# A state-space convolution on one core: x1 loads three channels ahead and late in SyncE's turn, Toeplitz loads first in it, k and B ahead of the transposes

## The chip, the cores and the metric

One core of one Trainium2 chip runs the whole program. The metric is the device time of one execution in microseconds (us), as the median of three runs. TensorE is called PE here, VectorE DVE, ScalarE ACT, GpSimd POOL and SyncE SP, as in the profile.

## The reference: what is computed

x has 128 batches, 128 channels and 2048 steps. Two residual layers follow each other:

```python
W = weights[condition]                      # (128, 128, 128): one of 16 matrices for each batch
x1 = x + jnp.einsum('bct,bcd->bdt', x, W)
mask = jnp.arange(L) < length[:, None]      # per batch
K = 2.0 * jnp.einsum('hn,hnl->hl', Cs, jnp.exp(P)).real     # (128 channels, 2048)
y = causal convolution of (x1 * mask) with K, channel by channel   # by FFT in the reference
out = x1 + (y + x1 * mask * D[:, None]) * mask
```

Everything is float32.

## The kernel before

**Rows.** The first layer works batch by batch ("rows"): 512 KB of x are loaded into `row_x`, multiplied by the matrix of the batch's condition (`w_sel`), copied to `row_y` and stored to `x1_scratch` in DRAM. The time axis is cut into two segments of 1024 steps. The 128 rows of segment 0 and four of segment 1 are made ahead of everything else. The other 124 rows of segment 1 are made one at a time beside the channels of segment 0 (`row_in_parts` on PE, `halve_w`, `halve_x` and `take_row` on ACT, `split_row` on POOL).

**Channels.** The second layer works channel by channel: 128 turns for segment 0, then 128 for segment 1. A turn k loads the channel's 128 batches x 1024 steps from `x1_scratch` into one of four tiles (512 KB, `load_x1`), transposes them on PE (`turn`), and splits them into a high and a low part (`keep_u` on ACT, `split_u` on DVE). PE then makes the chunk states from them (`drive`, `advance`), the near part with a Toeplitz matrix (`from_chunk`, with `t_hi`, `t_lo` and `toep`) and the far part from the states (`from_state`). `take_y` on DVE puts the result into the tile under the mask, and `store_x2` writes the tile to `out`. Tile, Toeplitz, b_mat and row_x buffers come in fours; `load_x1` waits for the store of the channel that had the tile four turns earlier.

**Matrices.** In segment 0 the kernel's taps k and the matrix B of channel k+2 are made in turn k: `make_mats` on PE, `keep_k`, `halve_k`, `split_k` on DVE, then `store_kernel` writes the taps to DRAM (72 KB). `load_toeplitz` reads them back in skewed form, three loads of 128, 128 and 64 KB, and waits for the landing of that store. B is split (`keep_b` on ACT, `split_b` on DVE) and stored by `store_b` (256 KB) for segment 1, which loads it with `load_b`. The last state of segment 0 goes to `edge_scratch` (line 402) and comes back by `load_edge` in segment 1.

**Order.** Each engine runs a list written out by hand, one turn after the other, and waits on semaphores. SP's list is also the order of the DMA queue on which all transfers but the `x1_scratch` stores (ACT's queue) are issued. A wait in SP's list holds up everything behind it. Which matrix a row needs is read by `act.value_load` into a register of ACT's sequencer (line 536).

Of the kernel before, what the change touches and what calls it, by code (L numbers as in the profile page):

```python
# [31 lines left out]
NCOND = 16  # L32
# [37 lines left out]
def s4d_program(nc, x, cond, length, weights, log_dt, c_in, log_a_real, a_imag, d_in, const_in, out):  # L70
# [10 lines left out]
    with ctx:  # L81
# [215 lines left out]
        def _(sp):  # L297
# [78 lines left out]
            for k in range(2):  # L376
                load_x1(0, k, k, 0)
# [3 lines left out]
            def channels(g, seg, with_rows):  # L381
                for j in range(SLOTS):
# [3 lines left out]
                    if then:  # L386
                        load_x1(then[0], then[1], j2, then[2])
                    if after and after[0] == 0:
                        if not (isinstance(k, int) and k == 0):
                            store_b(k + 1, j1)  # L390
                        load_toeplitz(0, k + 1, j1, after[2])
# [4 lines left out]
                    if with_rows and not (isinstance(g, int) and k + 3 >= B - AHEAD):  # L396
                        load_row(k + ROWS_FIRST + 3, j3, 1, k + AHEAD + 3)
                    if then and then[0] == 0:
                        store_kernel(k + 2, j2)
                    if seg == 0:  # L400
                        sp.wait_ge(s_ready, states_before(0, k) + NCH)
                        sp.dma_start(edge_dram[bass.ds(k, 1), :, :].rearrange("a n b -> (a n) b"), edge[j % 2][:, :]).then_inc(edge_saved[j % 2], 16)
# [107 lines left out]
        def _(act):  # L510
# [22 lines left out]
            def halve_w(m, j):  # L533

                n = m + ROWS_FIRST
                which = act.value_load(cond_sb[0:1, bass.ds(n, 1)], min_val=0, max_val=NCOND - 1)
# [87 lines left out]
            halve_w(0, 0)  # L624
# [3 lines left out]
            def channels(g, seg, with_rows):  # L628
                for j in range(SLOTS):
# [5 lines left out]
                    next_row = with_rows and not (isinstance(g, int) and k + 1 >= B - AHEAD)  # L635
                    keep_s(seg, k, j, 1)
                    if next_row:
                        halve_w(k + 1, j1)
                        halve_x(k + 1, j1, 0)
# [23 lines left out]
        def _(dve):  # L663
# [156 lines left out]
            def channels(g, seg, with_rows):  # L820
                for j in range(SLOTS):
# [7 lines left out]
                    if third:  # L829
                        mats(third[0], k + 3, (j + 3) % SLOTS)  # L830
                    if after:
                        split_u(k + 1, j1, 0)
                    if then and then[0] == 0:
                        keep_k(k + 2, j2)
# [18 lines left out]
        def _(pe):  # L853
# [99 lines left out]
            def channels(g, seg, with_rows):  # L953
                for j in range(SLOTS):
# [8 lines left out]
                    for c in range(NCH):  # L963
# [5 lines left out]
                        if c - 1 >= 1 - seg:  # L969
                            from_state(seg, k, j, c - 1)  # L970
                        if c == 0 and after:
# [3 lines left out]
                        if c == 0 and then and then[0] == 0:  # L975
                            make_mats(k + 2, j2)
# [50 lines left out]
```

## Time and profile before

| | us |
|---|---|
| median of 3 runs | 2345.85 |
| the runs | 2344.41 to 2353.0 |
| the profiled execution's own time | 2358.94 |
| its span, first to last instruction | 2357.1 |

The rows ahead of the channels take about 385 us of the span, segment 0 of the channels goes on to about 1510 us, and segment 1 fills the rest. PE is busy for 92% of the span, DVE 72%, ACT 64%, POOL 50%. The profiled execution is 13 us above the median of the runs.

### The profile page before, as it was taken

The numbers are of one execution on the slowest core, as the hardware profiler recorded it, in microseconds if no ns is written. First come the engines' busy times: TensorE is split into PE (matmuls) and PEld (weight loads), VectorE is DVE, ScalarE is ACT, GpSimd is POOL, SyncE is SP. The second block draws the span as 40 slices with busy tenths as digits, with TensorE's granted clock in tenths as the row PEclk, the third lists the DMA queues.
The fourth block names the chain that finished last, engine by engine and source line by source line (L and its number), as shares of the span: only waits on it lengthen the run. The fifth ranks groups of instructions, "written<-read, shape, count | busy, mean of one in ns | idle before, by whom it ended". The sixth has DMA issues, their size and how long they took to land.

```text
span 2357.1 us, 61717 instructions
## 1 busy us (share of the span) xinstructions
PE 2174.2 (92%) x15101; PEld 1880.7 (80%) x15101; DVE 1699.5 (72%) x3359; ACT 1505.9 (64%) x4354; POOL 1175.0 (50%) x1862
## 2 busy tenths in 40 slices
PE   6777778999999999999999999899999999999999
PEld 2222226888888888888888888799999999999998
DVE  4999204777777777777777777677777777777776
ACT  4556556777777777777777777455555555555555
POOL 0994503666666666666666666333333333333331
PEclk9999999999999999999999999999999999999999
DMA  8999999999999999999999999889989999899887
GB/s 319 420 414 369 394 359 330 316 315 315 314 316 318 317 317 318 320 315 317 320 319 311 323 316 307 241 251 262 268 253 267 266 270 259 259 261 264 254 260 223
DMA packets 337444, 716.26 MB, mean 304 GB/s; under 512 B 39554, under 2 KB 170884, under 8 KB 337412
## 3 DMA queue, kind: packets, MB, share of 16 engines
q1 hardware_dynamic: 300548, 581.66, 79.7%
q10 hardware_dynamic: 36864, 134.23, 14.0%
q8 instruction: 13, 0.21, 0.0%
q14 instruction: 19, 0.16, 0.0%
HBM read 395.92 MB, written 319.82 MB: 304 GB/s over the span
## 4 chain that ended last, share of the span: by engine, by line
PE 36%; DMA 28%; DVE 9%; SPq 8%; issue 8%; ACT 6%; ACTq 4%; DVEq 0%; POOL 0%
DMA decay<-x_scratch 12%; DMA toep<-k_scratch 11%; PE bank L900 7%; PE bank L902 6%; PE bank L901 6%; DMA row_x<-in_x 5%; PE bank L882 4%; DVE decay L803 4%; PE bank L945 4%; PE bank L869 3%; PE bank L937 3%; SPq L339 3%; SPq L355 2%; DVE e_lo L786 2%; ACTq L521 2%
## 5 line engine op out<-in xcount | busy, mean ns | idle before, releaser
L791 DVE TENSOR_TENSOR u_lo<-bank,u_hi 128x512 fp32r<-128x512 f32 x512 | 352.2, 688 | 252.7 <-ACT u_hi L603 246.7
L797 DVE TENSOR_TENSOR s_lo<-state,s_hi 128x128 fp32r<-128x128 f32 x768 | 291.8, 380 | 236.7 <-ACT s_hi L615 235.4
L900 PE MATMUL bank<-t_hi,u_hi 128*128 128x256 f32 x1024 | 361.7, 353 | 43.1 <-DMA toep<-k_scratch 42.5
L612 ACT ACTIVATE state<-bank 128x128 f32<-128x128 f32 x768 | 213.9, 279 | 286.8 <-PE bank L902 149.5
L803 DVE COPY_PREDICATED decay<-mask,bank 128x512 f32<-128x512 uint8 x512 | 379.1, 741 | 23.8 <-PE bank L902 3.6
L945 PE MATMUL bank<-toep,u_odd 128*128 128x128 f32 x2048 | 392.8, 273 | 0.0
L546 ACT ACTIVATE row_y<-bank 128x512 f32<-128x512 f32 x512 | 301.4, 589 | 138.2 <-ACT row_y L546 38.7
L489 POOL TENSOR_TENSOR x_lo<-row_x,x_hi 128x256 fp32r<-128x256 f32 x496 | 371.5, 778 | 0.0
L869 PE MATMUL bank<-row_x,w_sel 128*128 128x512 f32 x528 | 265.5, 630 | 94.2 <-DMA row_x<-in_x 50.2
L466 POOL TENSOR_TENSOR outer<-par 128x256 f32<-128x256 f32 x512 | 321.5, 649 | 20.5
L463 POOL COPY par<-table 128x71 f32 (+1 forms) x256 | 62.4, 244 | 540.4 <-PE bank L902 540.4
L945 PEld LDWEIGHTS bank<-toep,u_odd 128*128 128x128 f32 x2048 | 314.0, 189 | 0.0
L900 PE MATMUL bank<-e_hi,s_hi 128*128 128x256 f32 x896 | 307.3, 343 | 0.0
L869 PEld LDWEIGHTS bank<-row_x,w_sel 128*128 128x128 f32 x528 | 93.3, 195 | 263.7 <-ACT row_y L546 143.9
L603 ACT ACTIVATE u_hi<-bank 128x512 fp32r<-128x512 f32 x512 | 301.9, 590 | 0.0
L901 PE MATMUL bank<-t_lo,u_hi 128*128 128x256 f32 x1024 | 288.6, 282 | 0.0
L902 PE MATMUL bank<-t_hi,u_lo 128*128 128x256 f32 x1024 | 288.3, 282 | 0.0
L486 POOL TENSOR_TENSOR w_lo<-w_sel,w_hi 128x128 fp32r<-128x128 f32 x124 | 57.2, 461 | 423.0 <-ACT x_hi L529 423.0
L937 PE MATMUL bank<-state,r_mat 128*128 128x128 f32 x1280 | 265.5, 289 | 0.5 <-ACT state L612 0.4
L900 PEld LDWEIGHTS bank<-t_hi,u_hi 128*128 128x128 f32 x1024 | 195.8, 191 | 81.7 <-DMA toep<-k_scratch 65.7
L882 PE MATMUL bank<-eye_r,tile_r 128*128 128x128 f32 x2048 | 225.4, 253 | 34.1 <-DMA decay<-x_scratch 33.0
L615 ACT ACTIVATE s_hi<-state 128x128 fp32r<-128x128 f32 x768 | 238.6, 311 | 24.2
(139 smaller groups left out, 5456.6 us busy)
## 6 DMA issues: line engine op xcount, KB each, us to landing
row_x<-in_x SPq DMA_DIRECT2D x256, 512.0 KB, 6.1
x_scratch<-row_y ACTq DMA_DIRECT2D x256, 512.0 KB, 5.6
decay<-x_scratch SPq DMA_DIRECT2D x256, 512.0 KB, 6.4
out<-decay SPq DMA_DIRECT2D x256, 512.0 KB, 4.4
b_scratch<-b_mat SPq DMA_DIRECT2D x128, 256.0 KB, 6.5
t_hi<-k_scratch SPq DMA_DIRECT2D x256, 128.0 KB, 4.7
t_lo<-k_scratch SPq DMA_DIRECT2D x256, 128.0 KB, 4.4
b_mat<-b_scratch SPq DMA_DIRECT2D x128, 256.0 KB, 5.0
```

What stands on the lines that cost most here:

```text
L466: pool.tensor_tensor(outer[:, n, :].rearrange("p (a b) -> p a b", b=LOW), par[j][:, p0:p0 + LOW].unsqueeze(2).to_broadcast([P, LOW, LOW]), ...
L489: last = pool.tensor_tensor(x_lo[i][:, cols], row_x[j][:, cols], x_hi[i][:, cols].bitcast(fp32), ALU.subtract)
L603: nc.scalar.activation(u_hi[j % 2][:, 4 * q:4 * q + 4, :], blocks, ACT.Copy).then_inc(u_half, 1)
L791: v.tensor_tensor(u_lo[j % 2][:, blocks, :], t_bank[q][:, :].rearrange("s (k b) -> s k b", b=B), u_hi[j % 2][:, blocks, :].bitcast(fp32), ...
L803: v.copy_predicated(tile[j][:, cols], mask[:, seg * SEG + q * BANK:seg * SEG + (q + 1) * BANK], y_bank[q][:, :]).then_inc(y_taken, 1)
L869: mm(to_bank[:, :], w_sel[j][:, :], row_x[j][:, q * BANK:(q + 1) * BANK], start=True, stop=True).then_inc(row_made, 1)
L882: ins = nc.tensor.transpose(t_bank[q][:, n * P:(n + 1) * P].bitcast(fp32r), tile_r[j][:, at:at + P], eye_r[:, :])
L900: mm(to, w_hi, m_hi, start=start, stop=False, skip_group_check=True)
L901: mm(to, w_hi, m_lo, start=False, stop=False, skip_group_check=True)
L902: return mm(to, w_lo, m_hi, start=False, stop=stop, skip_group_check=True)
L937: mm(s_bank[j % 2][:, c * P:(c + 1) * P], r_mat[j][:, :], whole[:, :], start=False, stop=True, skip_group_check=True).then_inc(s_made, 1)
L945: mm(y[:, P:CHUNK], u_odd[i][:, c, :], toep[j][:, P - 1::-1], start=False, stop=True, skip_group_check=True)
```

## The change

SP: `load_x1` moves from the front of a turn to a place behind the kernel store, ahead of the edge and of `store_x2`, and loads the channel three ahead in place of two; three of them are issued ahead of the first turn. `load_toeplitz` comes first in a turn of segment 0, and `store_b` goes behind the row load. ACT: the condition is read ahead of the first state's copy. DVE: `keep_k` comes ahead of the first `split_u`. PE: `make_mats` comes ahead of the transposes. No work is added or removed.

```diff
--- before.py
+++ after.py
@@ -373,7 +373,7 @@
                 rows(g, 1)
             load_toeplitz(0, 0, 0, 0)
             sp.wait_ge(par_ready, 1)
-            for k in range(2):
+            for k in range(3):
                 load_x1(0, k, k, 0)
             for n in range(ROWS_FIRST, ROWS_FIRST + 3):
                 load_row(n, n % SLOTS, 1, n - B)
@@ -383,11 +383,7 @@
                     k = g * SLOTS + j
                     after, then, third = (later(g, j, seg, d) for d in (1, 2, 3))
                     j1, j2, j3 = ((j + d) % SLOTS for d in (1, 2, 3))
-                    if then:
-                        load_x1(then[0], then[1], j2, then[2])
                     if after and after[0] == 0:
-                        if not (isinstance(k, int) and k == 0):
-                            store_b(k + 1, j1)
                         load_toeplitz(0, k + 1, j1, after[2])
                     if then and then[0] == 1:
                         load_toeplitz(1, k + 2, j2, then[2])
@@ -395,8 +391,12 @@
                         load_b(k + 3, j3)
                     if with_rows and not (isinstance(g, int) and k + 3 >= B - AHEAD):
                         load_row(k + ROWS_FIRST + 3, j3, 1, k + AHEAD + 3)
+                    if after and after[0] == 0 and not (isinstance(k, int) and k == 0):
+                        store_b(k + 1, j1)
                     if then and then[0] == 0:
                         store_kernel(k + 2, j2)
+                    if third:
+                        load_x1(third[0], third[1], j3, third[2])
                     if seg == 0:
                         sp.wait_ge(s_ready, states_before(0, k) + NCH)
                         sp.dma_start(edge_dram[bass.ds(k, 1), :, :].rearrange("a n b -> (a n) b"), edge[j % 2][:, :]).then_inc(edge_saved[j % 2], 16)
@@ -530,10 +530,13 @@
                 if q == NQ - 1:
                     ins.then_inc(row_halved, 1)
 
-            def halve_w(m, j):
+            def condition_of(m):
+
+                return act.value_load(cond_sb[0:1, bass.ds(m + ROWS_FIRST, 1)], min_val=0, max_val=NCOND - 1)
+
+            def halve_w(m, j, which):
 
                 n = m + ROWS_FIRST
-                which = act.value_load(cond_sb[0:1, bass.ds(n, 1)], min_val=0, max_val=NCOND - 1)
                 act.wait_ge(row_made, n * NQ - NQ)
                 w = w_all[:, bass.ds(which, 1), :].rearrange("c k d -> c (k d)")
                 nc.scalar.activation(w_sel[j][:, :], w, ACT.Copy)
@@ -621,7 +624,7 @@
 
             for q in range(NQ):
                 keep_u(0, 0, q)
-            halve_w(0, 0)
+            halve_w(0, 0, condition_of(0))
             for q in range(NQ):
                 halve_x(0, 0, q)
 
@@ -633,9 +636,11 @@
                     if seg == 1:
                         halve_edge(k, j, g)
                     next_row = with_rows and not (isinstance(g, int) and k + 1 >= B - AHEAD)
+                    if next_row:
+                        which = condition_of(k + 1)
                     keep_s(seg, k, j, 1)
                     if next_row:
-                        halve_w(k + 1, j1)
+                        halve_w(k + 1, j1, which)
                         halve_x(k + 1, j1, 0)
                     if after:
                         keep_u(k + 1, j1, 0)
@@ -828,10 +833,10 @@
                     third = later(g, j, seg, 3)
                     if third:
                         mats(third[0], k + 3, (j + 3) % SLOTS)
+                    if then and then[0] == 0:
+                        keep_k(k + 2, j2)
                     if after:
                         split_u(k + 1, j1, 0)
-                    if then and then[0] == 0:
-                        keep_k(k + 2, j2)
                     split_s(seg, k, j, 2)
                     if then and then[0] == 0:
                         halve_k(k + 2, j2)
@@ -968,12 +973,12 @@
                         from_chunk(k, j, c)
                         if c - 1 >= 1 - seg:
                             from_state(seg, k, j, c - 1)
+                        if c == 0 and then and then[0] == 0:
+                            make_mats(k + 2, j2)
                         if c == 0 and after:
                             pe.wait_ge(x1_loaded[j1], after[2] * 16 + 16)
                             for q in range(NQ):
                                 turn(k + 1, j1, q)
-                        if c == 0 and then and then[0] == 0:
-                            make_mats(k + 2, j2)
                         if with_rows and c % 2:
                             row_in_parts(k, j, c // 2)
                     from_state(seg, k, j, NCH - 1)
```

In segment 0 SP's turn looks so before; `decay` is the tile that `load_x1` fills, `x_scratch` is what it reads. The rows are those of one turn near the end of the rows, from one store of `out` to the next.

```order
L324 DMA decay<-x_scratch 128x1024 [waits x2_stored2]
L355 DMA b_scratch<-b_mat 128x512 [waits b_ready]
L339 DMA t_hi<-k_scratch 128x1x256 [waits k_stored1]
L339 DMA t_lo<-k_scratch 128x1x256
L339 DMA toep<-k_scratch 128x1x128
L311 DMA row_x<-in_x 128x1024 [waits row_made]
L329 DMA k_scratch<-k_rows 16x1152 [waits k_ready]
L402 DMA edge_scratch<-edge 128x128 [waits s_ready]
L343 DMA out<-decay 128x1024 [waits y_taken]
```

After the change the same turn reads so. The tile's load has gone from the front to ahead of the edge, the three Toeplitz loads now open the turn, and the b store has gone behind the row's load.

```order
L339 DMA t_hi<-k_scratch 128x1x256 [waits k_stored1]
L339 DMA t_lo<-k_scratch 128x1x256
L339 DMA toep<-k_scratch 128x1x128
L311 DMA row_x<-in_x 128x1024 [waits row_made]
L355 DMA b_scratch<-b_mat 128x512 [waits b_ready]
L329 DMA k_scratch<-k_rows 16x1152 [waits k_ready]
L324 DMA decay<-x_scratch 128x1024 [waits x2_stored3]
L402 DMA edge_scratch<-edge 128x128 [waits s_ready]
L343 DMA out<-decay 128x1024 [waits y_taken]
```

In segment 1 one turn reads so on SP before, from the loop over the groups:

```order
L324 ISA [waits x2_stored2]
L324 DMA decay<-x_scratch 128x1024
...
L339 DMA t_hi<-k_scratch 128x1x256
...
L339 DMA t_lo<-k_scratch 128x1x256
...
L339 DMA toep<-k_scratch 128x1x128
...
L361 ISA [waits y_made]
L361 DMA b_mat<-b_scratch 128x512
...
L351 ISA [waits y_made]
L351 DMA edge<-edge_scratch 128x128
...
L343 ISA [waits y_taken]
L343 DMA out<-decay 128x1024
```

After the change the tile's load stands behind the b load and ahead of the edge's; its wait for the tile's earlier store stands there too, and the edge load and the out store are behind it.

```order
L339 DMA t_hi<-k_scratch 128x1x256
...
L339 DMA t_lo<-k_scratch 128x1x256
...
L339 DMA toep<-k_scratch 128x1x128
...
L361 ISA [waits y_made]
L361 DMA b_mat<-b_scratch 128x512
...
L324 ISA [waits x2_stored3]
L324 DMA decay<-x_scratch 128x1024
...
L351 ISA [waits y_made]
L351 DMA edge<-edge_scratch 128x128
...
L343 ISA [waits y_taken]
L343 DMA out<-decay 128x1024
```

ACT's list at the start of a turn of segment 0 before; TENSOR_LOAD is the read of the condition, and the state's copy is what PE's `advance` and DVE's `split_s` wait for.

```order
L550 DMA x_scratch<-row_y 128x1024
...
L612 ACTIVATE state<-bank 128x128 [waits s_made]
L615 ACTIVATE s_hi<-state 128x128 [waits s_ready]
...
L536 TENSOR_LOAD cond_sb
...
L539 ISA [waits row_made]
L539 ACTIVATE w_sel<-w_all 128x128
L540 ACTIVATE w_hi<-w_all 128x128
...
L529 ACTIVATE x_hi<-row_x 128x512 [waits x_loaded3]
```

After the change the read stands between the row's store and the state's copy, and the two copies of the matrix follow the state directly.

```order
L553 DMA x_scratch<-row_y 128x1024
...
L535 TENSOR_LOAD cond_sb
...
L615 ACTIVATE state<-bank 128x128 [waits s_made]
L618 ACTIVATE s_hi<-state 128x128 [waits s_ready]
...
L542 ISA [waits row_made]
L542 ACTIVATE w_sel<-w_all 128x128
L543 ACTIVATE w_hi<-w_all 128x128
...
L529 ACTIVATE x_hi<-row_x 128x512 [waits x_loaded3]
```

## Rows read from the trace of the kernel before

**Rows 1.** Busy time by stretch: PE, PEld, DVE, ACT, POOL, PEclk, DMA share, GB/s

```profile
100.00:200.00 100.00, 76.54 (x155) 26.05 (x155) 97.48 (x74) 53.64 (x116) 96.75 (x34) 1.00 1.02 409
700.00:1400.00 700.00, 675.36 (x4876) 608.11 (x4875) 529.99 (x1100) 510.98 (x1494) 452.65 (x788) 1.00 0.97 318
1600.00:2300.00 700.00, 678.47 (x5597) 667.98 (x5597) 530.24 (x1076) 408.43 (x1292) 240.00 (x431) 1.00 0.91 262
```

**Rows 2.** Waits in 700:1400: us in total, times, longest

```profile
PE bank L900 <- DMA toep<-k_scratch: 23.8, 38, 1.3
```

**Rows 3.** Waits in 1600:2300

```profile
PE bank L882 <- DMA decay<-x_scratch: 20.5, 29, 1.5
```

**Rows 4.** Issues of the out store in 700:1400, line 343: ns, first, last start

```profile
L343 SPq DMA_DIRECT2D out<-decay x79: 327/332/333, 700.8 to 1395.2; - x79
```

**Rows 5.** The same in 1600:2300, with its time to landing

```profile
L343 SPq DMA_DIRECT2D out<-decay x108: 360/361/361, 1600.6 to 2297.1; - x108
...
DMA to landing us min/median/max: 3.3/3.9/5.2
```

**Rows 6.** Timeline of SP, one turn of segment 0: start us, us

```profile
763.35 0.33 SPq L343 DMA_DIRECT2D out<-decay  x1
763.86 0.64 SPq L324 DMA_DIRECT2D decay<-x_scratch  x1
764.68 1.09 SPq L355 DMA_DIRECT2D b_scratch<-b_mat  x1
766.05 0.58 SPq L339 DMA_DIRECT2D t_hi<-k_scratch  x1
...
769.51 0.34 SPq L329 DMA_DIRECT2D k_scratch<-k_rows  x1
...
772.02 0.33 SPq L343 DMA_DIRECT2D out<-decay  x1
```

**Rows 7.** Timeline of SP, one turn of segment 1

```profile
1898.31 0.36 SPq L343 DMA_DIRECT2D out<-decay  x1
1898.95 0.34 SPq L324 DMA_DIRECT2D decay<-x_scratch  x1
...
1901.80 0.34 SPq L361 DMA_DIRECT2D b_mat<-b_scratch  x1
1903.56 0.33 SPq L351 DMA_DIRECT2D edge<-edge_scratch  x1
1904.45 0.36 SPq L343 DMA_DIRECT2D out<-decay  x1
```

**Rows 8.** Landing of the x1 load, line 324, in 1600:2300

```profile
DMA to landing us min/median/max: 4.7/6.2/7.7
```

**Rows 9.** Landing of the kernel store, line 329, in 700:1400

```profile
DMA to landing us min/median/max: 3.5/4.4/5.3
```

**Rows 10.** Landing of the Toeplitz loads, line 339, in 700:1400

```profile
DMA to landing us min/median/max: 3.6/4.5/5.9
```

**Rows 11.** Landing of the edge load, line 351, in 1600:2300

```profile
DMA to landing us min/median/max: 1.7/3.4/5.4
```

**Rows 12.** Timeline of ACT, segment 0: start us, us, idle before and releaser

```profile
905.65 0.28 ACT L612 ACTIVATE state<-bank 128x128 f32<-128x128 f32 x1 [1.15 <-PE bank L902]
...
907.06 0.31 ACT L539 ACTIVATE w_sel<-w_all 128x128 f32 x1 [0.79 <-issue]
...
909.04 0.28 ACT L612 ACTIVATE state<-bank 128x128 f32<-128x128 f32 x1 [0.20 <-PE bank L937]
```

**Rows 13.** Timeline of PE in the same turn

```profile
907.03 0.89 PE L882 MATMUL bank<-eye_r,tile_r 128*128 128x128 f32 x8
...
908.18 0.61 PE L895 MATMUL bank<-m_mat,e_mat 128*128 128x128 f32 x4
```

**Rows 14.** Timeline of PE where segment 1 begins

```profile
1518.20 0.96 PE L882 MATMUL bank<-eye_r,tile_r 128*128 128x128 f32 x8 [2.33 <-DMA decay<-x_scratch]
...
1528.88 1.16 PE L882 MATMUL bank<-eye_r,tile_r 128*128 128x128 f32 x8 [2.73 <-DMA decay<-x_scratch]
```

## The prediction

> **What bounds the kernel now.** I read the table by stretch first, for which engine is full; then the chain of waits by window, for what it waits for; then SP's timeline and the landings, for how late that is. In both stages of the channels PE is busy for 96 to 97% of the stretch at the full granted clock (1.00, its 2.4 GHz level), DVE for 76% and ACT for 73 and 58% [rows 1]. So PE is the bound, and what it waits for is the loss. In segment 0 that is the Toeplitz loads, 38 times in 79 turns, 23.8 us [rows 2]; in segment 1 it is the tile loaded from x1_scratch, 29 times in 108 turns, 20.5 us [rows 3].
>
> The rows of waits hold only whole gaps, so I take the loss from the period. The out stores of 79 turns of segment 0 are issued from 700.8 to 1395.2: 78 periods of 8.90 us [rows 4]. In segment 1 there are 107 periods in 696.5 us: 6.51 us [rows 5]. A turn without a wait takes 772.02 - 763.35 = 8.67 us in segment 0 [rows 6], and 1904.45 - 1898.31 = 6.14 us in segment 1 [rows 7]. Both are the commonest values of their stage: about half of the periods of segment 0 lie at or under 8.75, and 47 of 107 in segment 1 at or under 6.2, mostly every second one. The loss is 0.23 us x 124 turns = 29 us in segment 0 and 0.36 us x 126 = 45 us in segment 1. Where the segments meet, the tiles come late twice more, by 2.33 and 2.73 us [rows 14]: 5 us. At most 79 us, 3.4%, are to be had.
>
> The DMA engines are the second candidate. In the rows ahead of the channels they never idle, and the table gives a share of 1.02 at 409 GB/s. The channels have 0.97 and 0.91 [rows 1]. Against 1.02 as full, a turn of segment 0 needs 0.97 / 1.02 x 8.90 = 8.46 us of them and one of segment 1 needs 0.91 / 1.02 x 6.51 = 5.81 us. Both are under PE's 8.67 and 6.14, the first by only 2%.
>
> **Segment 1: the x1 load three ahead.** The load goes out 0.6 us behind the out store [rows 7] and lands 6.2 us later in the median, 7.7 at the worst [rows 8], so at 6.8 to 8.3. About half of the periods are lengthened, so the transposes of PE's next turn are due near the median landing, 6.8: there is no slack. Three ahead, there is a whole period more, 6.14 us. Against that stands that the load goes out later: behind the b load, which goes out 3.5 us into the turn [rows 7], and behind the landing of the store that frees the tile, issued at 0 and landing at 3.9, at worst 5.2 [rows 5]. So the load goes out at 4.0 to 5.3 in place of 0.6, and is due at 6.8 + 6.14 = 12.9. With 6.2 us to land it is there at 10.2 to 11.5: slack 2.7 us in the median and 1.4 with a late store, and only a landing that is late as well (1.5 over its median) uses it up. I keep 0.05 us of the 0.36 for such turns: -0.31 x 126 = -39 us. What is queued behind the new wait on SP: the edge load, which goes out at 5.25 [rows 7], and the out store. The wait ends at 4 to 5.3, so both go out as before. The two waits at the seam go too, since their loads are issued a turn earlier: -5 us.
>
> **Segment 0: the Toeplitz loads first.** They now go out 2.7 us into the turn, behind the x1 load and a b store whose issue alone takes SP 1.09 us [rows 6]. Put first, they go out at 0.5, if the kernel store has landed. It goes out at 6.16 (769.51 - 763.35) [rows 6] and lands 4.4 later, at worst 5.3 [rows 9]: 10.6 to 11.5, or 1.9 to 2.8 us into the next turn. Were nothing else changed, they would gain 0.8 us at best. But they also lose what is ahead of them on the queue: 512 KB of x1 and 256 KB of b, 1.9 us at 409 GB/s. Their landing of 4.5 us, at worst 5.9 [rows 10], is largely that queue. Together they land about 2.5 us earlier, against a longest wait of 1.3 [rows 2]. The wait goes. The DMA engines then have 8.46 of 8.67 us to work, so I don't book the whole 0.23: 0.18 x 124 = -22 us.
>
> **The rest.** The condition's read: ACT idles 0.79 us for it behind the state, and 1.15 us ahead of the state, waiting for PE [rows 12]. The read moves into that second gap; with the issue of the row's store in the same gap the state may come up to 0.4 us later. PE takes it only after the transposes and make_mats, 0.89 and about 1.0 us [rows 13], so nothing is booked, and ACT has its copies of u some 0.4 us earlier. PE's swap: the transposes come later by the length of make_mats, about 0.9 us [rows 13], and half of that is paid by the earlier ACT. The next state's copy has 0.20 us of idle time ahead of it [rows 12]. Between 0 and 0.15 us a turn may reach PE (0 to 19 us); I take 0, since the read's gain and the later transposes nearly meet. In DVE the taps' copy comes ahead of u, which uses the time it idles for u. The third x1 load ahead of the first turn delays the row loads behind it by 512 KB at 409 GB/s: +1 us.
>
> **At one place a page weighs otherwise.** The kernel store of 72 KB takes 4.4 us to land [rows 9]. The Trainium skill ("DMA: Bandwidth & Descriptors", "Anatomy of one DMA — SWDGE (gpsimd) path") gives a fixed cost of about 2.0 us plus bytes / 436e3 for one transfer on GpSimd's path, 2.2 us here, which is an estimate for another issuer. By it the store would be home before the turn ends and the Toeplitz loads would go out at 0.5, 2.2 us earlier than before, and by themselves remove the wait; by the row they wait for the store. The sum above goes by the row. No row here shows a lone store of this size.
>
> **Sum.** -39 - 5 - 22 + 1 = -65 us. The profiled execution took 2358.94 us and becomes 2294. It stands 13 us above the median of 2345.85. If the 13 us are of the kind that is removed, the new median is also about 2294 less a few; if they are the profiler's, it is 2281. I take 2286.
>
> **Rivals.**
> - *The DMA engines are the bound of segment 0.* For it: 8.46 of 8.67 us, and never more than a few unhindered turns in a row. Then the wait for Toeplitz loads turns into one for x1 or rows, segment 0 keeps 8.85 to 8.90, and segment 1, more crowded by the late x1 load, gains half: -20 - 5 = 2321. Against it: segment 1 has 11% of their time free. Chance 0.22.
> - *The kernel store's loop becomes the bound (slower).* Kernel store, landing, t_hi, the other loads, b store, next kernel store is a ring once per turn. From t_hi to the kernel store are 3.46 us, and the b store moved in between adds 1.37 (764.68 to 766.05) [rows 6]: 4.8. With 4.4 to land [rows 9] the ring is 9.2 us, over 8.67. If 256 KB of b directly ahead add 0.65 to the landing, it is 9.9: +1.0 x 124 = 124 us against -43 elsewhere, 2427. It decides from 9.25 us on, which is a landing of 4.45. Against it: the landing is time on the queue behind the row's load, and the x1 load and b store no longer stand ahead of these, so the queue is shorter by up to 1.9 us; at the lowest landing of 3.5 [rows 9] the ring is 8.3 and doesn't bind. Chance 0.08.
> - *The edge comes late in segment 1.* It now lies behind 512 KB of x1, 1.3 us at 409 GB/s, on top of 3.4, at worst 5.4 [rows 11]. It goes out at 5.25 and is due two turns' starts later, at about 12: slack 1.4 in the median, none in the worst. If it takes 0.25 us a turn, 2318. Chance 0.07.
> - *The waits are covered by others at once,* so that no part does what it says: 2345. Chance 0.05.
>
> **How the numbers follow.** The forecast has 0.58 and its own range 2267 to 2306: 79 us gained in full from 2346, and half of it. The range for 8 in 10 reaches over the DMA case and the edge: 2264 to 2322. A measurement of this kernel can tell about 0.5% from no change, 12 us: faster means under 2334. Forecast, edge and nearly all of the DMA case are there: 0.86. Within 0.5%: 0.07; slower: 0.07.
>
> **What would show it.** In the new trace the period of segment 0 is 8.70 to 8.75 and that of segment 1 about 6.2. The waits for toep and for decay<-x_scratch are a few us. t_hi goes out under 2 us behind the out store. The kernel store lands in under 4 us; over 4.5 would be the ring. A DMA share near 1.0 in segment 0 with a new wait for a load is the DMA case; a wait for the edge on ACT line 620 or PE's advance, the edge case. The prediction is wrong if PE's unhindered turn grows, by ACT or DVE, above 8.67.

## The result and the profile after

The changed kernel is slower, by 1.5%. Its median is 2383.66 us (four runs, 2378.92 to 2386.69) against 2348.11 us for the kernel before in the same comparison; the ratio is 1.0148, with a 95% interval of 1.0119 to 1.0177. Forecast were 2286 us, with a range of 2264 to 2322.

The profiled execution took 2378.92 us, its span 2377.1. Cut at the issues of the out store, the two spans differ as follows (before, after): up to the first out store 386.8 and 379.6 us; the first 124 turns of segment 0 1104.9 and 1145.0; the next four turns 34.1 and 33.6; the 127 turns of segment 1 828.2 and 815.8. So segment 1 gave back 12.4 us and segment 0 lost 40.1. The 7.2 us ahead of the first out store are no gain that can be read: between kernels whose code there is the same, that stretch took 380 us in one and 394 in another. The medians lie 35.5 us apart and the two spans 20, since the profiled execution of the kernel before was 11 us above its median and that of the changed kernel 5 us below.

The table by stretch, with the columns of [rows 1]; the second stretch starts a little later, since segment 1 does:

```profile
700.00:1400.00 700.00, 652.65 (x4682) 593.33 (x4680) 513.86 (x1060) 491.95 (x1439) 437.06 (x758) 0.99 0.93 304
1620.00:2320.00 700.00, 683.25 (x5635) 666.83 (x5635) 516.78 (x1083) 411.32 (x1301) 238.71 (x433) 1.00 0.88 264
```

In segment 0 every engine and the DMA engines are less busy than in [rows 1]: PE 653 us for 675, the DMA share 0.93 for 0.97. No engine is full, which points to waits that follow each other in a circle. The waits of 700:1400 (us in total, times, longest), where [rows 2] stood:

```profile
PEld bank L905 <- DMA toep<-k_scratch: 57.8, 42, 3.4
ACT u_odd L605 <- PE bank L887: 53.4, 44, 3.7
PE bank L905 <- DMA toep<-k_scratch: 45.7, 45, 2.9
```

PE waits for the Toeplitz loads longer than before, although they now stand first in SP's turn. They go out 3.45 us behind the out store in the median, where it was 2.59. Why they are late stands in SP's own waits, of the same stretch:

```profile
SPq L339 <- DMA k_scratch<-k_rows: 183.7, 73, 3.6
SPq L343 <- DVE decay L808: 30.5, 47, 1.1
SPq L329 <- DVE k_rows L783: 5.2, 9, 1.4
```

In 73 of some 76 turns SP stands at the first Toeplitz load (line 339), 2.5 us each time, until the kernel store of the turn before has landed. The same view of the kernel before shows that its SP hardly ever did:

```profile
SPq L329 <- DVE k_rows L778: 40.2, 71, 1.1
SPq L339 <- DMA k_scratch<-k_rows: 1.3, 3, 0.5
```

One turn on SP's timeline, beside [rows 6] (start us, us):

```profile
908.15 0.33 SPq L343 DMA_DIRECT2D out<-decay  x1
910.38 0.57 SPq L339 DMA_DIRECT2D t_hi<-k_scratch  x1
911.13 0.55 SPq L339 DMA_DIRECT2D t_lo<-k_scratch  x1
911.87 0.54 SPq L339 DMA_DIRECT2D toep<-k_scratch  x1
912.71 0.36 SPq L311 DMA_DIRECT2D row_x<-in_x  x1
913.26 0.35 SPq L355 DMA_DIRECT2D b_scratch<-b_mat  x1
913.87 0.33 SPq L329 DMA_DIRECT2D k_scratch<-k_rows  x1
914.42 0.37 SPq L324 DMA_DIRECT2D decay<-x_scratch  x1
915.47 0.34 SPq L402 DMA_DIRECT2D edge_scratch<-edge  x1
916.97 0.33 SPq L343 DMA_DIRECT2D out<-decay  x1
918.79 0.58 SPq L339 DMA_DIRECT2D t_hi<-k_scratch  x1
```

From t_hi at 910.38 to the kernel store at 913.87 nothing waits: 3.49 us of issuing. The next t_hi goes out at 918.79, 4.92 us after that store. This is one of the shorter turns; the median of the two parts over segment 0 is 3.52 and 5.65 us. And the landings have grown. Those of the kernel store and of the out store in 700:1400, the first of them where [rows 9] stood:

```profile
DMA to landing us min/median/max: 3.7/5.5/6.5
...
DMA to landing us min/median/max: 4.3/7.3/8.0
```

In segment 1 (1620:2320) the wait for the tile, [rows 3], is gone. In its place:

```profile
ACT s_hi L623 <- DMA edge<-edge_scratch: 156.5, 75, 3.2
PEld bank L942 <- DMA edge<-edge_scratch: 30.7, 45, 1.5
PE bank L942 <- DMA edge<-edge_scratch: 16.4, 33, 1.1
```

and on SP:

```profile
SPq L324 <- DMA out<-decay: 154.6, 103, 2.8
```

SP stands at the x1 load for the landing of an out store in nearly every turn, 1.5 us each time, and the edge load and the next out store stand behind it. That landing, where [rows 5] had 3.9 in the median:

```profile
DMA to landing us min/median/max: 4.0/5.0/6.4
```

### The profile page after: what moved, and what is told of

Read it like the earlier page. It is cut to its first block, busy times and chain, and to the rows that moved or that the text cites. A ratio compares the mean times of both kernels' runs of the same rounds, so it can differ in the third digit from the quotient of the medians.

```text
span 2377.1 us, 61746 instructions
## 1 busy us (share of the span) xinstructions
PE 2178.8 (92%) x15101; PEld 1889.3 (79%) x15101; DVE 1685.0 (71%) x3359; ACT 1505.1 (63%) x4354; POOL 1175.6 (49%) x1862
## 4 chain that ended last, share of the span: by engine, by line
DMA 38%; issue 20%; POOL 20%; SPq 9%; PE 6%; ACTq 2%; ACT 2%; POOLq 1%; DVE 0%; DVEq 0%
DMA out<-decay 26%; POOL x_lo L489 10%; DMA k_scratch<-k_rows 6%; POOL outer L466 5%; PE bank L874 4%; DMA row_x<-in_x 4%; POOL e_mat L471 3%; SPq L339 3%; SPq L324 2%; SPq L351 2%; ACTq L521 1%; POOL w_lo L486 1%; ACT row_y L549 1%; DMA x_scratch<-row_y 1%; ACTq L553 1%
## 5 line engine op out<-in xcount | busy, mean ns | idle before, releaser
L802 DVE TENSOR_TENSOR s_lo<-state,s_hi 128x128 fp32r<-128x128 f32 x768 | 271.1, 353 | 261.2 <-ACT s_hi L618 259.6
L605 ACT ACTIVATE u_odd<-bank 128x256 f32<-128x256 f32 x512 | 191.4, 374 | 131.4 <-PE bank L887 130.4
```

Source lines behind the costliest of these rows:

```text
L802: v.tensor_tensor(s_lo[c][:, :], whole[:, :], s_hi[c][:, :].bitcast(fp32), ALU.subtract).then_inc(s_split, 1)
```

## The experiments

Two theories were open, and both are told here by the ring that they name. **Ring one**, segment 0: t_hi, the other Toeplitz loads, the row load, the b store, the kernel store, its landing, and t_hi again. If it sets the time, then the period is the time from t_hi's issue to the kernel store's issue, plus the landing, plus SP's own step. **Ring two**, segment 1: the x1 load waits for the landing of the out store of the turn before; then come the x1 load, the edge load and the next out store. Its rival for segment 1 was a slower engine, and for segment 0 that ACT, PE or DVE came out slower by their edits.

The medians and ratios are those of each kernel's own comparison with the one before; "period" is that of segment 0 and of segment 1, from the out stores of the profiled execution; "issue" and "landing" are the medians of the two parts of ring one over the turns of segment 0 (in e9, e10, e12 and e13 ACT issues the kernel store, so there the first is no time on one list). A period is that of one execution; the issue part holds what SP waits for within it, above all DVE's taps. The kernel before had medians of 2348 to 2354 us in these comparisons, so kernels of different comparisons are compared by their ratios.

| kernel | median us | ratio to before | period 0 | issue | landing | period 1 |
|---|---|---|---|---|---|---|
| before | 2348 | | 8.91 | 3.59 | 4.41 | 6.52 |
| after | 2383.66 | 1.0148 | 9.23 | 3.52 | 5.49 | 6.42 |
| e1_engines_only | 2348.31 | 0.9977 | 8.86 | 3.37 | 4.67 | 6.48 |
| e2_sp_only | 2373.61 | 1.0099 | 9.16 | 4.48 | 4.43 | 6.44 |
| e3_b_behind | 2343.09 | 0.9951 | 8.89 | 2.98 | 5.58 | 6.47 |
| e4_x1_only | 2363.56 | 1.0050 | 9.08 | 4.33 | 4.55 | 6.44 |
| e5_x1_and_read | 2361.74 | 1.0040 | 9.07 | 2.98 | 5.86 | 6.45 |
| e6_x1_two_ahead | 2585.95 | 1.1007 | 10.33 | 4.16 | 5.91 | 6.92 |
| e7_edge_first | 2344.43 | 0.9979 | 8.84 | 2.98 | 5.59 | 6.49 |
| e8_x1_mid | 2541.27 | 1.0819 | 10.41 | 3.69 | 6.64 | 6.49 |
| e9_kstore_act | 2334.83 | 0.9934 | 8.93 | 3.15 | 5.52 | 6.37 |
| e10_kstore_out_act | 2331.91 | 0.9933 | 8.82 | 3.17 | 5.41 | 6.44 |
| e12_old_order_act | 2308.22 | 0.9846 | 8.85 | 3.17 | 4.47 | 6.20 |
| e14_x1_front | 2345.66 | 0.9976 | 8.78 | 3.53 | 5.09 | 6.52 |
| e13_b_behind_act | 2289.68 | 0.9736 | 8.69 | 3.17 | 5.21 | 6.23 |
| e15_b_behind_sp | 2282.53 | 0.9711 | 8.61 | 3.85 | 4.57 | 6.26 |

**e1: PE's, DVE's and ACT's edits alone, with SP as before.** (The edits of those three engines in the diff above, none of SP's.)

> The kernel before with only the edits of TensorE, VectorE and ScalarE (k and B ahead of the transposes, condition read first); SyncE's order as before. Ring theory (the loss sits in SyncE's ring kernel store, landing, Toeplitz loads, next kernel store): no ring here, so not slower than before: 2325 to 2350 us, an unhindered turn of segment 0 at 8.3 to 8.4 us in place of 8.67. Rival (the later transposes cost): slower than 2360 us.

The ratio is 0.9977 (0.9954 to 1.0000). The engines' edits don't cost anything. The commonest distance between two out stores of segment 0, the turn without a wait, fell from 8.66 to 8.32 us, which the prediction did not have; but the mean period stayed at 8.86, because the Toeplitz data comes when it came before. The waits of 700:1400:

```profile
PEld bank L905 <- DMA toep<-k_scratch: 45.4, 43, 2.1
PE bank L905 <- DMA toep<-k_scratch: 30.9, 40, 1.6
```

**e2: SP's edits alone.** (SP's hunks of the diff above.)

> The kernel before with only SyncE's edits. Ring theory: slow as the changed kernel, 2370 to 2400 us, periods of segment 0 at 9.2 to 9.3 us, SyncE waits over 2 us a turn at line 339 for the landing of the kernel store. Rival (the engines' edits cost): 2290 to 2340 us.

1.0099 (1.0066 to 1.0132), period 9.16. So the loss is SP's. Here the kernel store also waits for the taps, which DVE makes later than in the changed kernel, and the issue part is 4.48 us. So this ring runs through DVE as well. The waits of SP in 700:1400:

```profile
SPq L339 <- DMA k_scratch<-k_rows: 102.6, 68, 3.7
SPq L329 <- DVE k_rows L778: 67.4, 56, 1.9
```

**e3: the changed kernel with the b store behind the kernel store.**

> The changed kernel with the b store behind the kernel store, so that it leaves the ring and no 256 KB stand ahead of the kernel store. Ring theory: from the Toeplitz load to the kernel store 0.5 us less and a landing of 4.8 in place of 5.5 us; ring 8.1 us, period of segment 0 8.3 to 8.6, 2280 to 2310 us. Rival (the x1 load, next to the row store and the out store, crowds the queue and everything lands late): 2365 us or more, with the landing still over 5.2 us.

```diff
-                    if after and after[0] == 0 and not (isinstance(k, int) and k == 0):
-                        store_b(k + 1, j1)
                     if then and then[0] == 0:
                         store_kernel(k + 2, j2)
+                    if after and after[0] == 0 and not (isinstance(k, int) and k == 0):
+                        store_b(k + 1, j1)
```

0.9951 (0.9928 to 0.9973): some 40 us under the changed kernel, by one line moved, and between what was expected and what its rival would give. The issue part shrank by 0.54 us, the period by 0.34. The landing did not shrink: 5.58. SP still waits for it, less long, and a second wait has come up:

```profile
SPq L339 <- DMA k_scratch<-k_rows: 129.8, 76, 2.4
SPq L324 <- DMA out<-decay: 43.9, 69, 1.3
```

The second line is ring two in segment 0. The out store lands in 7.25 us, the x1 load goes out 0.16 behind that landing, and the next out store 1.36 behind the x1 load: 8.77 us, the median distance between two out stores. The changed kernel is close to it too: there the x1 load goes out 0.25 us behind the landing, although SP hardly waits for it (1.3 us in 76 turns). So whatever shortens ring one there gains a few tenths of a us a turn at most, until ring two holds the turn.

**e4 and e5: the kernel before with the x1 load three ahead and late, and the same with ACT's early read.**

> The kernel before with only the x1 load moved and three ahead; Toeplitz loads behind the b store, which opens the turn. Ring theory: the b store is not between the Toeplitz loads and the kernel store, so segment 0 is not slower than before (8.9 us or less); segment 1 as in the changed kernel (6.46); 2315 to 2345 us. Rival (the crowded x1 load costs): periods of segment 0 at 9.2 us, 2375 us or more.

> The kernel before with the x1 load late and three ahead, and ScalarE's condition read first. Theory R (with the x1 load late, segment 0 is held by ScalarE: its condition read grew from 0.58 to 1.02 us and TensorE waits for its state copies): period of segment 0 falls from 9.08 to 8.9 or less, 2330 to 2345 us. Rival (the DMA queue, crowded by the late x1 load, holds it): stays at 9.05 or more, 2360 us.

```diff
-                    if then:
-                        load_x1(then[0], then[1], j2, then[2])
...
                         store_kernel(k + 2, j2)
+                    if third:
+                        load_x1(third[0], third[1], j3, third[2])
```

The x1 load's move alone makes segment 0 slower: 1.0050 (1.0033 to 1.0067), 9.08. The wait for Toeplitz data is almost gone there (7 and 3 us in 78 turns), and PE waits for the state instead, 52 us at its weight loads, and ACT's read of the condition takes longer: its median went from 564 to 991 ns. Taking that read out of the way (e5) changed nothing: 1.0040, 9.07. The wait for the state went, and both rings took its place: 2.98 + 5.86 us in ring one, and 7.51 + 0.16 + 1.37 = 9.04 in ring two. The waits of SP in e5, 700:1400:

```profile
SPq L339 <- DMA k_scratch<-k_rows: 103.5, 72, 3.5
SPq L324 <- DMA out<-decay: 60.0, 68, 1.7
```

So the read alone was not what the x1 move costs. With it out of the way, the rings give nearly the same period.

**e6: the x1 load two ahead, right behind the Toeplitz loads.**

> The changed kernel with the x1 load two ahead again, right behind the Toeplitz loads; the ring (Toeplitz loads, row, b store, kernel store, landing) is as long in instructions. Theory C (the late x1 load piles up with the row store and the out store, and that lengthens the landing of the kernel store): landing 4.5 us in place of 5.5, ring 3.5 + 0.5 for the x1 load + 4.5 = 8.5, period of segment 0 8.6 to 8.8, 2315 to 2340 us. Theory B (only the b store in the ring counts): landing stays 5.4 us, 2375 us or more.

1.1007: far off what was expected. The x1 load now stands in ring one, and its tile is waited for as well; both parts grew, to 4.16 and 5.91. The waits of PE in 700:1400 show 63.6 us for the tile, in 55 of some 68 turns. e14 below asks for the tile as far ahead, from a place in front of the Toeplitz loads, outside the ring, and is at 0.9976. So the place in the list decides here, not the distance.

**e7: e3 with the x1 load behind the edge load in segment 1.** **e8: e7 with the x1 load ahead of the kernel store in segment 0.**

> The kernel with the b store behind the kernel store, and in segment 1 the x1 load behind the edge load. If the edge load, held in SyncE's list behind the x1 load's wait for the out store and queued behind its 512 KB, is what took the gain of segment 1, its wait goes, and the period falls from 6.47 to 6.2 to 6.3 us: 20 to 30 us faster than with the b store moved alone, 2315 to 2325 us. Rival (the DMA engines as a whole hold segment 1): stays at 6.45, with the wait for x1 or Toeplitz data in its place.

> As the run with the edge first, with the x1 load of segment 0 between the row load and the kernel store, away from the row store and the out store, and the b store behind the kernel store. Theory C: the out store lands in about 5 us in place of 7.2, the kernel store in 4.5; period of segment 0 8.4 to 8.6, 2270 to 2300 us. Rival (position on the queue does not matter, its total load does): period 8.9, 2320 us or more.

e7 traded one wait for the other. The wait for the edge on ACT fell from 165 us in e3 to 9 us, that of PE for the tile came back, and the period stayed at 6.49. The waits of PE in 1620:2320 are those of [rows 3] again, and SP still stands at the x1 load:

```profile
PE bank L889 <- DMA decay<-x_scratch: 20.2, 37, 1.2
...
SPq L324 <- DMA out<-decay: 133.7, 106, 2.2
```

The new order took the edge load out of ring two and left the ring closed: the out store now lands in 5.7 us, and with 0.16 and 0.63 us to the next one that is 6.5. So e7 could not bring segment 1 down.

e8 is far off what was expected: 10.41 us a turn. As in e6, the x1 load stands between the Toeplitz loads and the kernel store, inside ring one. Its landing is the longest, 6.64, and PE ran for 171 us of segment 0 at its 1.2 GHz level, against none there before.

**e9 and e10: the changed kernel with the kernel store issued by ACT; and with the out stores of segment 1 issued by ACT as well.**

> The changed kernel with the kernel store issued by ScalarE on its own DMA queue. Ring theory (a turn of segment 0 takes as long as from the first Toeplitz load to the next kernel store, plus that store's landing, because both stand in SyncE's list and the store waits in SyncE's queue): the landing falls from 5.5 to under 4 us, the wait of the Toeplitz loads to under 0.5 us a turn, the period from 9.23 to 8.4 to 8.6: about 90 us faster than the changed kernel, 2290 to 2310 us. Rival (the DMA engines are full, landings are long whatever the queue): landing 5 us or more, 2360 us or more.

> As the run before it, and in segment 1 the out stores issued by ScalarE too. Second ring (in segment 1 the x1 load waits in SyncE's list for the landing of the out store, and the next out store stands behind it: 5.0 + 1.4 = 6.4 us, the measured period): with the out store in another list the ring opens, the edge load is held only until y is made, and the period falls from 6.46 to 6.2 to 6.3: 20 to 30 us faster than the run before it, 2265 to 2285 us. Rival (the edge load behind 512 KB of x1 stays late, or the engines are full): 6.4 or more, no gain.

```diff
+                    if then and then[0] == 0:
+                        i = j2 % 2
+                        act.wait_ge(k_ready, k + 3)
+                        act.dma_start(k_dram[...], k_rows[i][...]).then_inc(k_stored[i], 16)
                     if seg == 0:
                         keep_s(seg, k, j, NCH)
```

On ACT's queue the kernel store lands in 5.52 us, as on SP's: the landing is not SP's queue. The period is now 8.93, where 8.4 to 8.6 were expected, and ring two is seen in segment 0 too: SP waits 1.3 us a turn at the x1 load for the landing of an out store. The waits of SP in e9, 700:1400:

```profile
SPq L339 <- DMA k_scratch<-k_rows: 136.8, 75, 3.7
SPq L324 <- DMA out<-decay: 100.6, 76, 4.5
```

The sum is that of a ring: out landing 7.17, then x1, edge and out issue, some 1.7, together 8.9 against a period of 8.93. The 1.7 hold some waiting for DVE, and SP still waits for the kernel store as well, so here the two rings are not told apart. In e10 the out store is off SP in segment 1, yet the gain that was expected there did not come. The x1 load still waits for its landing (5.8 us), and the edge load behind it is still late:

```profile
ACT s_hi L629 <- DMA edge<-edge_scratch: 189.4, 95, 4.0
```

The edit has in fact made another ring, two turns long, since ACT issues an out store right behind its copy of the edge. The medians round it are: landing of the out store 5.77 us, x1 load 0.17 later, edge load 0.59 later, its landing 5.79, the out store of two turns later 0.35 behind that. Together they are 12.67 us, and two turns take 12.77. So e10 does not show that a late x1 load is worth nothing.

**e12: SP's old order and the engines' edits, with the kernel store and the out stores of segment 1 issued by ACT.** In segment 1 this leaves hardly a wait for a tile's store on SP, and no out store ahead of the x1 load there. (One group of the loop is written out for it, as in e10, e13 and e15.)

> SyncE's old order (x1 load two ahead, first in the turn) with the new order of the other engines, and the kernel store and the out stores of segment 1 on ScalarE's queue. If the late x1 load is worth something once the rings are open, this is slower than the run before it: 2310 to 2330 us, with waits for Toeplitz data in segment 0 and for x1 in segment 1. If not, it is as fast as that one.

```diff
-                    store_x2(seg, k, j)
+                    if seg == 0:
+                        store_x2(seg, k, j)
...
                     if seg == 1:
                         halve_edge(k, j, g)
+                        store_out(g * SLOTS + (j - 1), (j - 1) % SLOTS)
```

0.9846 (0.9811 to 0.9881). Segment 1 runs at 6.20 us a turn, against 6.15 for its shortest turns. In segment 1 e12 differs from e1 only in who issues the out stores, and e1 has 6.48. In segment 0 it differs only in who issues the kernel store, and there 8.86 and 8.85 are the same. SP's timeline there, for two turns, beside [rows 7]:

```profile
1902.77 0.33 SPq L352 DMA_DIRECT2D edge<-edge_scratch  x1
1903.79 0.33 SPq L325 DMA_DIRECT2D decay<-x_scratch  x1
1904.44 0.57 SPq L340 DMA_DIRECT2D t_hi<-k_scratch  x1
...
1909.03 0.33 SPq L352 DMA_DIRECT2D edge<-edge_scratch  x1
1909.55 0.33 SPq L325 DMA_DIRECT2D decay<-x_scratch  x1
```

SP no longer stands at an out store for DVE's last step, so the x1 load, still two ahead, goes out earlier in PE's turn. The slack of the tile, from its landing to PE's first transpose of it, is now 1.96 us in the median, where it was 0.12. It was late by SP's list, not by its distance in channels.

**e14: the changed kernel with the x1 load at the front of the turn, two ahead.**

> The changed kernel with only the x1 load back at the front of SyncE's turn and two ahead. The ring has the same instructions as in the changed kernel (3.6 us from the first Toeplitz load to the kernel store). Pile theory (the late x1 load, beside the row store and the out store, is what lengthens the landings): the kernel store lands in 4.4 to 4.7 us and the out store in under 5, the ring is 8.2 and does not bind, period of segment 0 8.7 to 8.85, 2325 to 2345 us. Rival (the b store ahead of the kernel store lengthens its landing): landing 5.3 us or more, period 9.1 or more, 2370 us or more.

```diff
+                    if then:
+                        load_x1(then[0], then[1], j2, then[2])
                     if after and after[0] == 0:
                         load_toeplitz(0, k + 1, j1, after[2])
...
-                    if third:
-                        load_x1(third[0], third[1], j3, third[2])
```

This is the clean test of the x1 load's place. The issue part of ring one is the same (3.53 for 3.52); the landing went from 5.49 to 5.09 and the period from 9.23 to 8.78. The out store lands in 5.9 us instead of 7.3. The kernel store's landing in 700:1400:

```profile
DMA to landing us min/median/max: 4.3/5.1/6.1
```

It came down less far than expected, so the x1 load's place is not the whole of it. The ratio is 0.9976 (0.9954 to 0.9997). The profiled execution was the fastest of ten, 12 us under their median, but the ratios give nearly the same step: 40 us between this kernel and the changed one, and 12 more that segment 1 loses here, are 0.42 us for each turn of segment 0.

**e13 and e15: e12 with the b store behind the row load; and with the kernel store back on SP, ahead of the b store.** (The first hunk and the last two lines are e13's, the kernel store's two lines e15's.)

> SyncE's old place of the x1 load, Toeplitz loads right behind it, b store behind the row, kernel store and the out stores of segment 1 on ScalarE's queue, new order of the other engines. If segment 0 is held by the late Toeplitz data alone (they go out 1.3 us earlier here), its period falls from 8.85 to 8.5 to 8.65, 2270 to 2290 us. Rival (the DMA engines hold it, at 0.96 of the stretch): 8.8, 2300 us or more.

> As the run before it, with the kernel store on SyncE ahead of the b store. Ring 3.1 + 4.5 us = 7.6, not binding: as fast as the run before it within 10 us. Rival (the kernel store's own queue matters): 20 us or more slower.

```diff
                     if after and after[0] == 0:
-                        if not (isinstance(k, int) and k == 0):
-                            store_b(k + 1, j1)
                         load_toeplitz(0, k + 1, j1, after[2])
...
+                    if then and then[0] == 0:
+                        store_kernel(k + 2, j2)
+                    if after and after[0] == 0 and not (isinstance(k, int) and k == 0):
+                        store_b(k + 1, j1)
```

0.9736 (0.9700 to 0.9772) and 0.9711 (0.9672 to 0.9750). e15 is the fastest kernel of the study, 2282.53 us. The kernel store lands in 4.57 us there and in 5.21 in e13, where it comes from ACT behind the b store. In e15 SP waits for it in 54 of 81 turns, 0.7 us each; the store itself waits for DVE's taps, so SP's list alone no longer closes the ring. Its landing and the waits of SP in 700:1400:

```profile
DMA to landing us min/median/max: 3.6/4.5/5.8
...
SPq L344 <- DVE decay L818: 79.0, 81, 1.1
SPq L330 <- DVE k_rows L793: 58.1, 80, 1.1
SPq L340 <- DMA k_scratch<-k_rows: 40.2, 54, 1.7
```

## Why the prediction was wrong

**What was right.** PE was the bound, and the loss in the two segments was there to be had: segment 1 was brought to 6.20 to 6.26 us a turn (e12, e15), segment 0 to 8.61. The best kernel gained 2.9%, where at most 3.4% were counted. DMA as the bound of segment 0 was not the case: its share fell to 0.93 as the period grew, and e15 has 0.99 at 8.61 us.

**Segment 0, -22 us booked, +40 measured.** The step that failed is the landing of the kernel store. The prediction says of the Toeplitz loads "they also lose what is ahead of them on the queue", and of the kernel store that "the queue is shorter by up to 1.9 us; at the lowest landing of 3.5 [rows 9] the ring is 8.3 and doesn't bind". That landing grew from 4.4 to 5.5 us. The Toeplitz loads did land faster, in 3.9 us for 4.5, but they went out 3.45 us behind the out store and not under 2, since SP stood there for the kernel store.

Ring one was named as a rival and got 0.08. By the prediction's own terms it stood at 9.2 us, over the 8.67 of a turn without a wait and over the 8.90 of the kernel before, and should have counted as the bound. "It decides from 9.25 us on" has no ground in its rows. That 9.2 is close to the measured 9.23 is luck: the issue part was put at 4.8 us and is 3.52, the landing at 4.4 and is 5.49. Of the 4.8, the b store in its new place takes SP 0.6 us and not 1.37, and the 3.46 of [rows 6] held about half a us of waiting for DVE's taps, which is gone with the earlier `keep_k` (SP waited 40.2 us for them in 700:1400 before, 5.2 after, and 67.4 in e2, which has the new order on SP but not that edit).

The table and SP's waits show ring one as the bound. In the changed kernel, e6, e8 and e14 the issue part holds almost no wait (at most 5.2 us in 700:1400), and SP stands for the landing in nearly every turn. Issue and landing add up to 9.01, 10.07, 10.33 and 8.62 us there, and the periods are 9.23, 10.33, 10.41 and 8.78: the sum and 0.1 to 0.3 us. In e2 and e15 the sums, 8.91 and 8.42 for 9.16 and 8.61, hold waits for the taps; in e3, e5 and e7 ring two is closed beside ring one. In before, e1 and e12 the sum is 7.6 to 8.0 and the period stays at 8.85 to 8.91, so ring one does not set it.

The Trainium skill ("DMA: Bandwidth & Descriptors", "Anatomy of one DMA — SWDGE (gpsimd) path") says that DMA engines don't wait on semaphores, and that a wait is spent on the issuing sequencer ahead of the dispatch. The trace agrees: SP stands 2.5 us at line 339 and nothing behind it is issued.

**Why the landing grew** is shown in part. e9 excludes SP's queue (5.52 us on ACT's), and e3 excludes the b store as the only cause (5.58 without it ahead). e14 shows that the x1 load's late place gives 0.40 us of the 1.1. The b store right ahead of the kernel store gives 0.52: in segment 0, e14 and e15 differ only in that, 5.09 against 4.57 and 8.78 against 8.61 us a turn. Together that is nearly the 1.1. But the two don't add in every order: e3 has the x1 load's late place without the b store ahead, and lands in 5.58; e4 has the late place too, and lands in 4.55.

Two explanations that lie near don't hold. The late x1 load is not more crowded by the x1_scratch store and the out store: before, the three go out within 1.2 us, with the x1 load behind the out store, and after the change within 1.8 us, with the x1 load ahead of it. And the amount in flight doesn't give the landing. Worked out from the traces in 700:1400: when a kernel store goes out, 1600 KB are issued and not landed in the median, before (it lands in 4.4 us) as after the change (5.5). For an out store it is 1224 KB before (4.7 us), 1416 in e15 (5.3), 1480 in e14 (5.9) and 1992 in the changed kernel (7.3), but 1672 in both e4 and e5, which land in 6.5 and 7.5, and 1928 in both e2 and e3, which land in 6.3 and 7.3. So what a landing is in a given order stays open. What e4 and e14 do show is that moving the x1 load late costs segment 0 0.17 us a turn by itself, or 0.45 where the Toeplitz loads come first.

**Segment 1, -39 us booked, -12 measured.** The tile's slack rose as reckoned, from 0.12 to 1.36 us, and it is never late. The step that failed is "The wait ends at 4 to 5.3, so both go out as before". It took the landing of the out store from [rows 5], 3.9 us; it is 5.0 now. With the x1, edge and out issues behind it, some 1.4 us, that is 6.4 us, and the period is 6.42: ring two. SP waits for nothing else there. The edge's slack, from its landing to PE's first use, is 0.35 us in the median, and under 0.2 in 44% of the turns. Its rival had 0.07, and its price of 0.25 us a turn is about the measured one; but its slack of 1.4 us doesn't come out of its own terms (12 - 5.25 - 1.3 - 3.4 is about 2), and the cause that it names, 512 KB ahead, is only a part beside the wait for the out store. e12 shows that the size of the loss was right: 0.32 us a turn are gained once the out store is off SP's list, with the x1 load in its old place.

**The seam, -5 booked.** The four turns there took 34.1 us before and 33.6 after, but the second late tile of [rows 14] falls into the first turn of segment 1, which took 10.2 us and takes 6.3. PE's waits for the tile are gone at the seam. Over eight turns it went from 63.5 to 58.1 us, so this term was right, and about 4 us of the 12 in segment 1 are its own. **The third x1 load, +1:** not to be told apart. **The engines' edits, 0 booked:** e1 is within 0.5% of the kernel before, but not because the read's gain and the later transposes meet: the turn without a wait fell by 0.34 us, and this was hidden by the Toeplitz loads. With these early enough it counts, and e15's 8.61 lies under the 8.67 that was taken as PE's floor.

**The clock.** Waits of PE of 1.8 to 2.9 us in the changed kernel are followed by stretches at the 1.2 GHz level: 37.5 us of them in segment 0, none there before. The mean granted clock over the span is 0.985, and was 0.994. How much of the 40 us this is was not measured apart. An estimate from these rows: at half the clock 37.5 us cost 19 us if PE was busy throughout, and less where it waited for the ring anyway.

**What stays open:** the 0.3 us a turn between e15's 8.61 and the unhindered 8.32. PE's weight loads and matmuls still wait 28.5 and 15.7 us for the Toeplitz data there in 700:1400, and the DMA share is 0.99. An issue of the Toeplitz loads from another engine was not tried.

## What to carry to other kernels

Where an issuing list waits for the landing of a transfer that the same list issued a turn earlier, add up issue time and landing round the ring before you move anything: if the sum lies near the period, what is moved into the ring, or beside the transfer whose landing counts, becomes the bound. Take that landing at its worst, not at its best: it isn't only what stands ahead of it on its own queue, and here neither the queue nor the amount in flight foretold it. Look for the next ring too: where two have nearly the same sum, opening one gains only their difference. Asking for a tile further ahead in a fixed set of buffers brings the wait for the buffer with it; taking the out stores off the list that is late did more here.

## What the runs showed of the hardware

A store of 72 KB took 4.4 to 6.6 us in the median to land, by the order of the transfers round it, and 5.5 us on either of two queues (after, e9). It took 4.4 us before and 5.5 after the change with the same 1600 KB in flight at its issue. A store of 512 KB took 4.7 us before and 7.5 in e5. ACT's read of one number (TENSOR_LOAD) took 564 ns in the median before and 991 ns in e4, where it stands behind the state, and 282 (e1), 283 (e5), 323 (the changed kernel) and 438 ns (e3) where it was moved ahead of the state.
